# Neighbour gather dealt 5, 9, 7, 9 over four tile slots, and the order of GpSimd's work changed with it

## What is computed

```
xx = jnp.sum(p * p, axis=1)
pd = 2.0 * jnp.einsum('bdn,bdm->bnm', p, p) - xx[:, :, None] - xx[:, None, :]
idx = jax.lax.top_k(pd, k)[1]
rel = pts[bidx, idx] - pts[:, :, None, :]
rho, theta, phi  from rel            (sqrt, arctan2)
att = softmax(lrelu(bn(W3 ... lrelu(bn(W1 feat)))))
out = x + einsum('bnkc,bnk->bnc', x[idx], att)
```

## Time and profile before

| | us |
|---|---|
| median of 3 runs | 5790.62 (5788.26 to 5792.64) |
| the profiled execution | 5790.79 |
| its span | 5788.7 |
| VectorE busy | 5127.8 (89%) |
| TensorE busy | 4476.3 (77%) |
| ScalarE busy | 4035.6 (70%) |
| GpSimd busy | 3045.6 (53%) |

### The profile page before, as it was taken

The page is one execution under the profiler, slowest core; times in us unless marked ns, Lnnn a source line. Parts: engine busy times, 40 slices in busy tenths (PEclk is TensorE's granted clock), DMA queues, the critical chain, the costliest instruction groups (busy, mean ns, idle before and its releaser), DMA issues. The chain is left out here.

```text
span 5788.7 us, 168877 instructions
## 1 busy us (share of the span) xinstructions
PE 4476.3 (77%) x62610; PEld 2718.6 (47%) x63182; DVE 5127.8 (89%) x7549; ACT 4035.6 (70%) x9505; POOL 3045.6 (53%) x3780
## 2 busy tenths in 40 slices
PE   5777777777777777777777777776395889999999
PEld 2444444444444444444444444443242666666666
DVE  7999989999989999998999998997398988888887
ACT  3777777777777777777777777776533766676666
POOL 3577777777777777777777777776400000000000
PEclk7888888888888898888888888887697899999999
DMA  0010000010000001000001000000000000000000
GB/s 29 16 31 16 16 17 16 17 31 16 17 16 17 17 16 32 16 17 16 17 17 31 17 16 17 16 16 12 1 0 8 25 30 27 30 26 30 26 30 26
DMA packets 135798, 114.60 MB, mean 20 GB/s; under 512 B 105344, under 2 KB 106112, under 8 KB 134784
## 3 DMA queue, kind: packets, MB, share of 16 engines
q1 hardware_dynamic: 134912, 102.73, 6.1%
HBM read 69.16 MB, written 33.55 MB: 18 GB/s over the span
## 5 line engine op out<-in xcount | busy, mean ns | idle before, releaser
L866 DVE MAX8 vals<-pd_sb 128x8 f32<-128x1024 f32 x1024 | 1200.6, 1211 | 302.2 <-ACT pd_sb L588 284.0
L588 ACT ACTIVATE ohT<-oh_ps 128x512 bf16<-128x512 f32 x1920 | 1152.0, 615 | 155.3 <-PE oh_ps L482 114.4
L871 DVE FIND_INDEX8 idx<-vals,pd_sb 128x8 uint16<-128x1024 f32 x1024 | 1244.6, 1218 | 0.0
L503 PEld LDWEIGHTS g_ps<-tparts,ohT 128*128 128x128 bf16 x23040 | 871.8, 99 | 380.9 <-issue 148.7
L503 PE MATMUL g_ps<-tparts,ohT 128*128 128x24 bf16 x23040 | 883.9, 175 | 81.6 <-issue 33.5
L873 DVE MATCH_REPLACE8 pd_sb<-vals,pd_sb 128x1024 f32<-128x1024 f32 x768 | 928.3, 1209 | 0.0
L1957 PEld LDWEIGHTS e_a_ps<-planes,e_oh 120*128 120x128 bf16 x24576 | 687.9, 97 | 299.5 <-issue 218.4
L482 PE MATMUL oh_ps<-bitsT,code 128*128 128x512 bf16 x1348 | 590.3, 442 | 293.4 <-ACT bitsT L772 155.7
L1727 ACT COPY e_at<-e_a_ps 128x512 f32<-128x512 f32 x512 | 543.1, 1061 | 356.1 <-PE e_a_ps L1957 349.8
L1957 PE MATMUL e_a_ps<-planes,e_oh 120*128 120x32 bf16 x24576 | 702.4, 178 | 83.2 <-DVE e_oh L1885 46.9
L754 ACT ACTIVATE sS<-s_ps,mx 128x64 f32<-128x64 f32 x2048 | 611.5, 329 | 169.4 <-DVE mx L896 168.1
(11 more groups left out here) (241 smaller groups left out, 7411.3 us busy)
## 6 DMA issues: line engine op xcount, KB each, us to landing
ctx_s<-in_ctx SPq DMA_DIRECT2D x32, 512.0 KB, 4.2
maskb<-in_mask_Bx1x_ff SPq DMA_DIRECT2D x32, 512.0 KB, 6.7
x_s<-in_x SPq DMA_DIRECT2D x32, 512.0 KB, 5.8
y_spill<-y_s SPq DMA_DIRECT2D x32, 512.0 KB, 3.0
e_y<-y_spill SPq DMA_DIRECT2D x32, 512.0 KB, 3.9
out<-e_o SPq DMA_DIRECT2D x64, 256.0 KB, 2.2
table<-in_ctx SPq DMA_DIRECT2D x96, 4.0 KB, 5.8
pd_sb<-in_shape_constants SPq DMA_DIRECT2D x1, 1180.0 KB, 5.4
```

Source lines behind the costliest of these rows:

```text
L503: m = nc.tensor.matmul(found_ps[gi % 2][:, k % GK, t, :], ohT[:, k % OHR, bass.ts(t, P)], tparts[:, par, part, :], start=(part == 0), stop ...
L588: return nc.scalar.activation(dst, src, func, scale=scale, bias=bias)
L866: nc.vector.max(vals[:, i, :], pd_sb[:, (t + i) % RING, :]).then_inc(topk_step, 1)
L871: found = nc.vector.max_index(idx16[:, par, t + i, 8 * r:8 * r + 8], vals[:, i, :], work)
```

## The change

The units get a table `units_at` with seven places per slot: 5, 9, 7 and 9 units in the four slots of a half; in the first slot none stands ahead of either half of the distances. On ScalarE `rel_squares` and `angles` move from slot 2 to slot 1, `roots` from slot 4 to slot 5. On VectorE `denoms` moves from rank 1 to behind rank 3 of the last pair. On GpSimd the groups are dealt (4, 5), (0), (1), (2, 3); `sph_turn` and `sph_signs` move from slot 3 to slot 2, `sph_denoms` from slot 5 to slot 6, and `squares_split` from slot 4 to slot 5, behind `rows`.

```diff
-        unit_starts = (0, 7, 15, 22, 30)
-        slot_groups = [(4, 5), (0,), (1, 2), (3,)]
+        units_at = ((0, 0, 1, 1, 1, 1, 1),
+                    (1, 1, 1, 1, 1, 2, 2),
+                    (1, 1, 1, 1, 1, 1, 1),
+                    (1, 1, 1, 1, 1, 2, 2))
+        unit_starts = [sum(sum(row) for row in units_at[:n]) for n in range(QT + 1)]
+        slot_groups = [(4, 5), (0,), (1,), (2, 3)]
...
(TensorE and ScalarE, the same shape in both)
-                    unit()
-                    ahead(0)
-                    unit()
-                    ahead(1)
-                    unit()
+                    units(0)
+                    ahead(2, 0)
+                    units(1)
+                    ahead(2, 1)
+                    units(2)
...
(ScalarE)
-                    if t == 2:
+                    if t == 1:
                         if there(b - 3):
                             angles(b - 3)
                         if there(b - 2):
                             rel_squares(b - 2)
-                    if t == 4 and there(b - 2):
+                    if t == 5 and there(b - 2):
                         roots(b - 2)
...
(VectorE)
-                        if t == 6 and r == 1 and there(b - 2):
+                        if t == 6 and r == 3 and there(b - 2):
                             denoms(b - 2)
...
(GpSimd)
                     if t == QT + 1:
                         rows(b, j, par, 0, misc_base(b) + (15 if first else 20))
+                        if not last:
+                            gate(pool, y_ready, b * 2 + 1, pool_gates)
+                            squares_split(b + 1, 1 - par, misc_base(b) + (12 if first else 16))
...
-                    if t == 3:
+                    if t == 2:
                         if there(b - 3):
                             sph_turn(b - 3)
                         if there(b - 2):
                             sph_signs(b - 2)
-                    if t == 5 and there(b - 2):
+                    if t == 6 and there(b - 2):
                         sph_denoms(b - 2)
...
                         invert(b + 1, (b + 1) // 2 if isinstance(b, int) else (j if par == 0 else j + 1), 1 - par)
-                        squares_split(b + 1, 1 - par, misc_base(b) + (12 if first else 16))
+                        gate(pool, minv_ready, b + 2, pool_gates)
```

More of the change, by code:

```diff
@@ L513, in emit, with units, ahead @@
                     at = unit_starts[quarter]
-                    end = unit_starts[quarter + 1]
-                    def unit():
+                    def units(place):
                         nonlocal at
[L518 to L525, removed]
+                        n = units_at[quarter][place]
+                        if not first and n > 0:
+                            gather(b - 1, 1 - par, h, at, at + n, turned)
+                        at += n
+                    def ahead(tiles, half):
+                        if t + tiles < TILES:
+                            distances(b, par, t + tiles, half)
                         elif not last:
-                            distances(b + 1, 1 - par, t + 2 - TILES, half)
+                            distances(b + 1, 1 - par, t + tiles - TILES, half)
                     before = t > 0 or not first
@@ L560, in emit @@
                         norms(misc, b + 1, 1 - par)
[L561 to L562 removed]
+                    units(6)
             def rows(misc, moved):
@@ L676, in emit, with units, ahead @@
                     at = unit_starts[quarter]
-                    end = unit_starts[quarter + 1]
-                    def unit():
+                    def units(place):
                         nonlocal at
[L681 to L687, removed]
+                        n = units_at[quarter][place]
+                        if not first and n > 0:
+                            gather(b - 1, h, at, at + n)
+                        at += n
+                    def ahead(tiles, half):
+                        if t + tiles < TILES:
+                            distances(b, par, t + tiles, half)
                         elif not last:
-                            distances(b + 1, 1 - par, t + 2 - TILES, half, normed)
+                            distances(b + 1, 1 - par, t + tiles - TILES, half, normed)
                     before = t > 0 or not first
@@ L696, in emit @@
                         bits(mv_)
-                    unit()
-                    ahead(0)
+                    units(0)
+                    ahead(2, 0)
                     exponents(b * TILES + t, t)
[L700 to L703, removed]
+                    units(1)
+                    ahead(2, 1)
+                    units(2)
+                    units(3)
                     if before:
                         turned_probs(mv_)
-                    unit()
+                    units(4)
                     if before:
                         values(mv_, (t - 1) % TILES)
-                    unit()
+                    units(5)
                     if quarter == 0 and before:
```

9 lines of the change are left out of this document (5 added, 4 removed).

## The result

| | before | after |
|---|---|---|
| median of the runs taken together (lowest to highest) | 5789.44 us (5787.87 to 5792.64) | 5875.93 us (5857.98 to 5877.47) |
| ratio, 95% interval | | 1.0141 (1.0125 to 1.0157) |
| span of the profiled execution | 5788.7 us | 5874.1 us |
| one batch of stage a | about 125.4 us | about 128.2 us |

The change makes the kernel 1.4% slower, 86 us. The forecast was 5776 us, with a range up to 5845: wrong in sign and outside the range.

A forecast was written before the change was run, and what follows sets the result against it. VectorE, 89% busy, bounds it, waiting once a batch at tile 7. Saved 11.0 us against `pT` 10.2 later: mean 1.1 earlier, less charges 0.3 and 0.3, 0.5 x 30 = 15 us less than 5790.79: 5776, range 5700 to 5845.

The forecast's parts named there:

- The mechanism: GpSimd, slot 2: sign steps and group 2 delay spread keys, `normalise` of tile 2 and `gsb`; `pT` 10.2 us later.
- The wait at tile 7: VectorE, last pair of each batch: its wait of about 8 us for tile 7's distances stays.
- from the second half to the end of `vz`: ScalarE after tile 6's second half: 12.5 us, with waits for GpSimd inside, becomes 8.8 on slot 0's model; saves 3.6.
- the sum: Savings from `pT` to tile 7, even batch: 4.3, 0.45, 3.6, 1.9 and 1.4, less 0.7, 11.0 us in all.
- the charge of 0.3 for the clock: Charge (b), TensorE: idling before `pT` lowers its clock, squares behind `pT` slow by 0 to 1.1 us, taken as 0.3.
- Charge (a): GpSimd in `sph_signs`: VectorE's digits before the conversion slow it by 0 to 1.0 us per batch, taken as 0.3.
- Costed at nothing: Moves of `squares_split`, `denoms`, `rel_squares` and `angles`, SP's queue and slot 7's late group 2: covered, so no cost.
- B: Rival: stalls put TensorE at 1.2 GHz, tile 7 2.0 us later than before; plus 60 us, 5851; chance 0.25.
- C: Rival: tile 3 misses 28.2, up to 1 us wait in half the batches; 15 us more, 5791; chance 0.05.
- A: Rival: GpSimd does not hold `pT`; gain 147 us, 5644, or nearer form 5731; chance 0.18 with its near form.

The follow-up runs named there:

- the division alone: Changed kernel with only the 16 sign steps divided, 8 in slot 2 (with the turn) and 8 in slot 3: 5657.7 us, 0.978.
- the kernel of 5568 us: Changed kernel with the signs divided over slots 2 and 3 and groups (1, 2) and (3,) back, first split of the norms still late: 5568.32 us, 0.9628.
- the deal alone: Kernel before with only the new table of units on TensorE and ScalarE, nothing else moved: 5785.11 us, 0.9988.

## Why the prediction was wrong

**The mechanism was right up to `pT`.** Forecast, against the trace of the odd batch shown and, in brackets, of the even batch before it: the scores of tile 4 at 59, 58.8 (59.4); `normalise` of tile 2 done at 61.6, 61.5 (62.1); `pT` at 66.55, 66.2 (66.8); the wait at `gsb` some 4 us, 3.21. By the ruler `pT` moved 10.4 us, forecast 10.2. The wait at tile 7 stays, at 6.5 us.

**The step that failed is the term "from the second half to the end of `vz`",** 12.5 us cut to 8.8 on the model of slot 0. It measured 11.9 in the odd batch shown (2272.52 to 2284.39) and 11.0 in the even one before it. Stretch by stretch, from `pT` on (the forecast takes the same for both kinds of batch):

| stretch | before, even | forecast | measured, odd | measured, even |
|---|---|---|---|---|
| `pT` to tile 6, first half | 12.6 | 9.0 | 9.6 | 9.2 |
| tile 6, first to second half | 3.4 | 2.9 | 2.9 | 2.9 |
| tile 6, second half, to tile 7, first | 15.9 | 10.4 | 13.4 | 12.5 |
| tile 7, first to second half | 4.8 | 3.4 | 3.4 | 3.4 |

Three of four are right within 0.6 us; the third is short by 2.1 and 3.0. In the mean of batches 7 to 19 the way from `pT` to the second half of tile 7 fell from 37.2 to 28.5 us: 8.7 saved, where the sum had 11.0 and set it against 10.2. This is why tile 7 comes 1.8 us later and not 1.1 earlier.

The runs split the term. That the waits for GpSimd inside it would go was right: with the old deal of units in the changed kernel it is 8.0 us, slot 0's length to the tenth. What the new deal adds was mis-sized: 0.85 us in the sum (two one-hots less a copy), 3.2 measured (8.0 to 11.2 between two kernels that differ in the deal alone, means of batches 7 to 19). The deal takes the one-hots from in front of the distances of slot 4, which gives 3.7 us there (13.1 to 9.5), and gives nearly all of it back behind them: ScalarE stands 2.72 us before a one-hot (`2277.79`) while TensorE does the scores of tile 5 ahead of it, at 1.98 us for the four matmuls of L449. Slot 0 of the earlier trace rows had one-hots in front of its distances, and no slot had the new order.

Part of that is TensorE's clock. Windows of TensorE (stretch, then length, busy us of each engine, and the granted clock, third from the end):

```profile
2252.00:2253.00 1.00, 0.37 (x2) 0.15 (x2) 1.00 (x2) 0.00 (x0) 1.00 (x2) 0.50 0.00 0
...
2275.00:2277.00 2.00, 2.00 (x6) 0.29 (x4) 0.00 (x0) 0.07 (x1) 0.24 (x1) 0.50 0.03 8
```

That is 1.2 GHz after 6.14 us of idle time in front of the first. The squares of L394, a part of slot 3's work, took 3.09 us, 2.15 before. In another batch of the same kernel the scores of tile 5 ran at the full clock of 2.4 GHz:

```profile
1116.71 1.08 PE L449 MATMUL s_ps<-kz,qs 128*64 128x512 f32 x4
...
1117.00:1119.00 2.00, 2.00 (x25) 1.04 (x22) 1.17 (x2) 0.68 (x2) 1.31 (x2) 1.00 0.00 0
```

There the third stretch was 11.4 us. In the 13 batches from 7 to 19 it was 13.4 in the five whose scores took 1.98, and 11.4 to 12.5 in the others. So 1 to 2 of the 3.0 us in the batch shown go with slow matmuls at that place; the charge of 0.3 for the clock was of the right kind and too small. No run changed the clock alone.

**A due time was not looked at.** The forecast followed the late keys to the scores of tile 4 and found them in time for their row maxima. It followed the late `pT` to the distances of tiles 6 and 7, but not to what stands between the halves of tile 6: the exponent of tile 4, and behind it the scores of tile 5. Their maxima are the 93.1 us. The forecast's own times would have shown it: second half of tile 6 at 78.4, a unit and 1.1 to 2.0 us of scores behind it, and VectorE there at 79.5. This wait is not a loss on top: it stands in front of the one at tile 7 and takes its place. Together they are 341.9 - 302.2 = 39.7 us more than before, tile 3 included.

**Charge (a) was put on the wrong engine.** It gave GpSimd 0.3 us a batch for digits beside its steps. The loser was VectorE, 1.3 us a batch (38 us), and at the other digits of the batch, beside the spread keys, which the forecast left out since only their time moves, not their place in the order. With the 1.8 us by which tile 7 is later this makes the loss: 3.1 us a batch in the batches of the ruler, 2.8 over the run.

**"Costed at nothing":** `squares_split` held its cover (TensorE's wait at L401 is 14.0 us in all) and later proved a gain of 39 to 68 us, which no term had, even where the batch is shorter and TensorE does wait at L401 (120.4 us with the division alone). `rel_squares` and `angles`, moved to slot 1, cannot be told apart here: no run moved them alone, and what `roots` and `denoms` bring alone was not tried either.

**The rivals.** B (slower by 60 us through TensorE's clock) had the nearer number, and its mechanism is in part there, at the squares and at the scores of tile 5, not at the distances of tile 6. It is not the main cause. The edit that divides the signs also ends TensorE's long wait for the spread keys (182.8 to 2.8 us), so by its total alone it would not rule B out; but in that kernel the squares behind `pT` are as slow (3.39 us in the batch shown), the way behind `pT` is only 0.7 us shorter in the mean (27.8 against 28.5), and 6.7 of the 7.2 us are `pT` itself. C (tile 3 misses its time) came true, and larger than priced. Timeline of VectorE of the changed kernel, a later batch:

```profile
2867.14 1.23 DVE L869 MAX8 vals<-pd_sb 128x8 f32<-128x1024 f32 x1 [3.48 <-ACT pd_sb L592]
```

Eleven batches have such a wait, up to 3.59 us, 25 us in all, where 15 were priced. A (GpSimd does not hold) was the opposite of the truth. That its 147 us of gain lie near the 125 us by which the division leaves this kernel under the one before is chance: it comes from taking half of GpSimd's block away from `pT`.

**Where the 218 us were.** The change put `normalise` of tile 2, two spread keys and group 2 behind one block of 15.7 us. The prediction had this chain in numbers, summed it against the savings and found them nearly equal. It took the block as given. The sum itself said what to do: each us off that block is worth about 30.

## What to carry to other kernels

When four engines answer one another in fixed order, price a block of low-priority work by what stands behind it in both slots it could go to, and divide it before moving it whole. Follow a late result to every deadline, through what stands behind it in each engine's order, not only to its first reader. Work taken from in front of a late result comes back behind it: price it there by the waits that it opens, not by its own length. After any change of timing look again at the mean of instructions that did not change: two engines that hold each other up can pay back a gain in a place that no edit touched.

## What was not expected of the hardware

VectorE's digits split with one 128x120 16-bit operation took 0.29 to 0.30 us when GpSimd was idle at its start, and else what was left of GpSimd's instruction and 0.16 us more, up to 2.00 us: so in 27 of 28 cases in the changed kernel and 13 of 13 in the one before. The three digit operations took together 2.41 us in the mean before, 3.04 after and 2.19 in the kernel of 5568 us: between the ends 0.85 x 61 = 52 us a run. For the deal alone they made 45 us less waiting a gain of 7. GpSimd, coming second, lost less in the one place looked at: 1.42 for 1.04 us, behind an instruction of VectorE with 0.53 us left.
